# A 16-bit permutation turned by DMA transposes instead of TensorE, in a graph kernel whose engines run pair by pair

## The reference

```python
mask = (adj > 0.0).astype(x.dtype)
W1a, W1b = (W1[:F], W1[F:])
xj_proj = x @ W1a
diff = x[:, :, None, :] - x[:, None, :, :]
h = jax.nn.relu(xj_proj[:, :, None, :] + diff @ W1b + b1)
hm = jnp.einsum('bjkh,bjk->bjh', h, mask)
deg = jnp.sum(mask, axis=-1)
return hm @ W2 + deg[..., None] * b2
...
x = _layernorm(x + _L0_gnn_ref(x, adj, ...), axis=-1)
```

## Time and profile before

| | us |
|---|---|
| median of three runs | 252.81 |
| the profiled execution | 252.74 |
| its span, first to last instruction | 250.9 |
| PE busy | 235.9 (94%) |
| DVE busy | 226.6 (90%) |
| ACT busy | 209.8 (84%) |
| POOL busy | 121.4 (48%) |
| DMA, mean of 16 engines | 21.7% of the span |

### The profile page before, as it was taken

The page is one execution under the profiler, slowest core; times in us unless marked ns, Lnnn a source line. Parts: engine busy times, 40 slices in busy tenths (PEclk is TensorE's granted clock), DMA queues, the critical chain, the costliest instruction groups (busy, mean ns, idle before and its releaser), DMA issues. The chain is left out here.

```text
span 250.9 us, 9244 instructions
## 1 busy us (share of the span) xinstructions
PE 235.9 (94%) x2810; PEld 188.7 (75%) x2813; DVE 226.6 (90%) x778; ACT 209.8 (84%) x572; POOL 121.4 (48%) x288
## 2 busy tenths in 40 slices
PE   7947989999999999999999999999999999998992
PEld 2524758888787878787888878887878888886761
DVE  4757699999999999999999999999999999997763
ACT  2384888989998989899899999898999989987631
POOL 1124444363645637463736364563736483576225
PEclk9985899999999999999999999999999999999998
DMA  6983003221212213131313021221310110000002
GB/s 201 357 325 106 3 4 123 70 84 30 70 54 78 73 55 96 44 107 42 106 39 107 14 74 59 64 82 47 105 44 25 43 46 0 25 24 1 3 8 63
DMA packets 10550, 18.20 MB, mean 73 GB/s; under 512 B 1296, under 2 KB 7696, under 8 KB 10512
## 3 DMA queue, kind: packets, MB, share of 16 engines
q1 hardware_dynamic: 10512, 17.73, 21.7%
HBM read 15.63 MB, written 2.10 MB: 71 GB/s over the span
## 5 line engine op out<-in xcount | busy, mean ns | idle before, releaser
L1327 PE MATMUL ring<-hot,vh 128*128 128x128 bf16 (+9 forms) x768 | 117.4, 255 | 1.3 <-ACT ring L914 1.0
L1327 PE MATMUL ring<-hot,vl 128*128 128x128 bf16 (+9 forms) x768 | 116.3, 251 | 0.0
L1796 DVE SCALAR_TENSOR_TENSOR sums<-ring,sums 128x256 f32<-128x256 f32 (+10 forms) x240 | 97.8, 428 | 4.3 <-PE ring L1327 1.9
L1327 PEld LDWEIGHTS ring<-hot,vh 128*128 128x128 f16 (+1 forms) x768 | 62.0, 104 | 23.6 <-issue 16.8
L1327 PEld LDWEIGHTS ring<-hot,vl 128*128 128x128 f16 (+1 forms) x768 | 61.9, 103 | 2.4
L661 POOL TENSOR_TENSOR vl<-vf,vh 128x384 f16<-128x384 f32 x32 | 29.7, 929 | 63.2 <-ACT vf L870 59.4
L903 ACT COPY ring<-u_sb 128x192 f32<-128x192 f32 (+8 forms) x160 | 49.3, 359 | 7.4 <-DVE sums L1796 7.4
L900 ACT COPY ring<-u_sb 128x512 f32<-128x512 f32 (+1 forms) x80 | 43.3, 559 | 0.4 <-issue 0.2
L715 POOL TENSOR_TENSOR sums<-taken,sums 128x512 f32<-128x512 f32 x16 | 20.7, 1292 | 27.1 <-ACT taken L932 27.1
L821 ACT CAST maskT<-bx 128x512 bf16<-128x512 f32 x32 | 18.5, 586 | 14.3 <-PE bx L1171 13.8
L1771 DVE TENSOR_SCALAR hot<-slotT 128x944 bf16<-128x944 f16 (+6 forms) x112 | 28.6, 280 | 0.0
(11 more groups left out here) (119 smaller groups left out, 463.7 us busy)
## 6 DMA issues: line engine op xcount, KB each, us to landing
adj_sb<-adj SPq DMA_DIRECT2D x16, 512.0 KB, 3.7
x_sb<-x_pairs SPq DMA_DIRECT2D x16, 128.0 KB, 2.3
xT_sb<-xT SPq DMA_DIRECT2D x16, 128.0 KB, 2.1
x_all<-x SPq DMA_DIRECT2D x4, 512.0 KB, 7.9
out<-o_sb SPq DMA_DIRECT2D x16, 128.0 KB, 1.7
wts<-weights SPq DMA_DIRECT2D x1, 417.0 KB, 4.8
cst_general<-general SPq DMA_DIRECT2D x1, 256.0 KB, 3.2
cst_half<-half SPq DMA_DIRECT2D x1, 137.0 KB, 3.1
```

The costliest lines, as they stand in the source:

```text
L1327: return eng.matmul(to if part == "main" else to[g * HT:g * HT + HT], values, selection, start=False, stop=final, skip_group_check=True)
L1796: eng.scalar_tensor_tensor(out=to, in0=view(pair, part, unit, piece), scalar=0.0, in1=to, op0=ALU.max, op1=ALU.add).then_inc(added[part], 1)
```

## The change

DVE writes the permutation as bf16 (`perm16`), and `rank` is f16. ACT widens `perm16` to the f32 `perm` that `sort_x` needs (`widen_perm`, new). The four tiles of `perm16` are transposed by four DMAs, SBUF to SBUF, that SP issues with `transpose=True` into `permT16` (`turn_perm`, now on SP); ACT widens it to `permT` as before, now from SBUF. PE's `turn_perm`, the bf16 identity go. The PSUM bank `bx3` loses one user, so `project` and `excess_main` wait for `sums_started` where they waited for `permT_copied`. The orders of the tasks are changed on all five queues. The core of the diff:

```diff
-        rank = sb("rank", [P, TILES])
-        perm = both("perm", [P, TILES, P])
-        permT = both("permT", [P, TILES, P])
+        rank = sb("rank", [P, TILES], F16)
+        perm16, perm = both("perm16", [P, TILES, P], BF16), both("perm", [P, TILES, P])
+        permT16, permT = both("permT16", [P, TILES, P], BF16), both("permT", [P, TILES, P])
```

On SP:

```diff
+            def perm_to_turn(pair):
+                eng.wait_ge(perm_ready, pair.n + 1)
+
+            def turn_perm(pair):
+                for c in range(TILES):
+                    eng.dma_start(permT16[pair.side][:, c, :], perm16[pair.side][:, c, :],
+                                  transpose=True).then_inc(permT_landed[pair.side], 16)
...
             def body(pair, has=always):
+                if has(1):
+                    perm_to_turn(new)
+                if has(3):
+                    load_x(third)
+                if has(1):
+                    turn_perm(new)
                 if has(5):
                     load_adj(fifth)
                 if has(4):
                     load_xT(fourth)
-                if has(3):
-                    load_x(third)
                 if has(-1):
                     store(old)
```

On ACT:

```diff
+            def widen_perm(pair):
+                eng.wait_ge(perm_ready, pair.n + 1)
+                if pair.follows(2):
+                    eng.wait_ge(xs_ready, pair.n - 1)
+                eng.copy(perm[pair.side][:, :, :].rearrange("p c r -> p (c r)"),
+                         perm16[pair.side][:, :, :].rearrange("p c r -> p (c r)")).then_inc(perm_widened, 1)
...
             def copy_permT(pair):
-                eng.wait_ge(permT_ready, pair.n + 1)
+                eng.wait_ge(permT_landed[pair.side], 16 * TILES * (pair.half + 1))
...
                     full_v(pair, 0)
                 if has(-1):
+                    copy_permT(old)
                     seed(old, "main", 4)
...
                 if has(1):
+                    widen_perm(new)
                     copy_maskT(new, 0)
                     copy_maskT(new, 1)
                 if has(-1):
                     seed_joint(old)
-                if has(0):
-                    copy_permT(pair)
```

On PE:

```diff
             def sort_x(pair):
...
-                eng.wait_ge(perm_ready, pair.n + 1)
+                eng.wait_ge(perm_widened, pair.n + 1)
...
-            def turn_perm(pair):
...
-                eng.wait_ge(sums_started, pair.n + 1)
...
-                to = bx3.bitcast(BF16)
-                for c in range(TILES):
-                    last = eng.transpose(to[:, c * P:c * P + P], perm16(pair.side, c), ident[:, :])
-                last.then_inc(permT_ready, 1)
...
             def body(pair, has=always):
-                    gather(pair, "main", 6, 3, 4)
                     gather(pair, "tail", 3)
...
-                if has(2):
-                    turn_perm(second)
...
-                    gather(new, "main", 6, 0, 3)
+                    gather(new, "main", 6)
```

In the start-up of PE:

```diff
             hidden_u_main(Pair(0, 0))
             hidden_u_tail(Pair(0, 0))
+            excess_main(Pair(0, 0))
             spread_x()
+            set_banks(0)
             hidden_v(Pair(0, 0))
+            keys(Pair(0, 1))
             set_banks(1)
```

In the end of PE:

```diff
             gather(Pair(0, 15), "tail", 0)
+            gather(Pair(0, 15), "main", 0)
+            gather(Pair(0, 15), "main", 1)
             gather(Pair(0, 15), "tail", 1)
-            gather(Pair(0, 15), "main", 0)
-            keep_busy_last(7)
-            gather(Pair(0, 15), "main", 1)
...
+            project(Pair(0, 15))
+            unsort_y(Pair(0, 15))
             add_over()
-            project(Pair(0, 15))
+            keep_busy_last(7)
             keep_busy_last(2)
-            unsort_y(Pair(0, 15))
```

On DVE:

```diff
             def permutation(pair):
-                eng.tensor_tensor(perm[pair.side][:, :, :], places.unsqueeze(1).broadcast_to([P, TILES, P]),
+                eng.tensor_tensor(perm16[pair.side][:, :, :], places.unsqueeze(1).broadcast_to([P, TILES, P]),
                                   rank[:, :].unsqueeze(2).broadcast_to([P, TILES, P]), ALU.is_equal).then_inc(perm_ready, 1)
```

More of the change, by code:

```diff
@@ L433, in build @@
         general_step = sem("general_step")
-        def perm16(side, c):
-            return perm[side][:, c, :].bitcast(BF16).rearrange("p (r two) -> p r two", two=2)[:, :, 1]
         def bank(pair, part, unit):
@@ L558, in _ @@
             load_adj(Pair(0, 3))
+            perm_to_turn(Pair(0, 0))
             load_x(Pair(0, 2))
+            turn_perm(Pair(0, 0))
             load_xT(Pair(0, 2))
             load_adj(Pair(0, 4))
+            perm_to_turn(Pair(0, 1))
             load_x(Pair(0, 3))
+            turn_perm(Pair(0, 1))
             load_adj(Pair(0, 5))
@@ L572, in general @@
                 load_xT(pair)
+                perm_to_turn(pair)
                 load_x(pair)
+                turn_perm(pair)
                 store(pair)
@@ L740, in body @@
                     low_v(new, 0)
-                    low_v(new, 1)
                 if has(-2):
                     scale(older)
+                if has(1):
+                    low_v(new, 1)
                 if has(2):
@@ L877, in copy_permT @@
                 eng.copy(permT[pair.side][:, :, :].rearrange("p c n -> p (c n)"),
-                         bx3.bitcast(BF16)[:, 0:TILES * P]).then_inc(permT_copied, 1)
+                         permT16[pair.side][:, :, :].rearrange("p c n -> p (c n)")).then_inc(permT_copied, 1)
             def copy_y(pair):
@@ L1097, in general @@
             def general(pair):
+                widen_perm(pair)
                 for g in range(2):
@@ L1171, in turn_masks @@
                         last = eng.matmul((bx1, bx2)[g][:, at:at + P], mask[pair.side][:, g * NT + t, k * P:k * P + P],
-                                          perm16(pair.side, g * NT + t), start=True, stop=True)
+                                          perm16[pair.side][:, g * NT + t, :], start=True, stop=True)
                 last.then_inc(maskT_ready, 1)
@@ L1191, in number_slots @@
                             last = eng.matmul(b[:, at:at + P], least[pair.side][:, g, t * (NT + 1):t * (NT + 1) + 1].to_broadcast([P, P]),
-                                              perm16(pair.side, c), start=False, stop=True)
+                                              perm16[pair.side][:, c, :], start=False, stop=True)
                 last.then_inc(slots_ready, 1)
@@ L1282, in project @@
                         eng.wait_ge(z_added, PAIRS - 1)
-                    eng.wait_ge(permT_copied, pair.n + (1 if pair.last() else 2))
+                    eng.wait_ge(sums_started, pair.n + (1 if pair.last() else 2))
                 for step in range(first, end):
@@ L1484, in _ @@
             gather(Pair(0, 0), "main", 5)
-            turn_perm(Pair(0, 1))
             number_slots(Pair(0, 2), 0)
@@ L1566, in general @@
                 eng.wait_ge(general_step, (pair.data + 1) * (N * GENERAL_STEPS))
-                turn_perm(pair)
                 project(pair)
@@ L1642, in ranks @@
                         eng.wait_ge(above_ready, pair.n)
-                eng.tensor_reduce(rank[:, :], steps_ahead[:, :, :], AX.X, ALU.add).then_inc(ranks_ready, 1)
+                with nc.allow_low_precision(reason="whole numbers of at most 128"):
+                    eng.tensor_reduce(rank[:, :], steps_ahead[:, :, :], AX.X, ALU.add).then_inc(ranks_ready, 1)
             def permutation(pair):
@@ L1899, in body @@
                     select(old, 9)
+                if has(-2):
+                    add(older, "tail", 7)
                 if has(0):
@@ L1946, in body @@
                     masks(second)
+            first_max()
             masks(Pair(0, 0))
```

236 lines of the change are left out of this document (112 added, 124 removed).

## The result

The changed kernel takes 257.29 us (median of four runs, 257.15 to 257.61) against 253.03 for the kernel before in the same comparison: 1.0164 times as long, with a 95% interval of 1.0132 to 1.0196. That is 4.3 us slower. The forecast was 250.6 with a range of 248.6 to 254.8, and faster was the likeliest sign. The prediction was wrong, in sign too.

The account below looks back on a forecast made before the run. It took PE as going at its own pace, 13.60 us busy of 13.6 per pair, with DVE less than 1% behind. Terms -2.3 + 0 + 0.3 + 0 + 0.5 - 0.7 = -2.2 us gave 250.6, range 248.6 to 254.8.

Parts of the forecast that it names:

- Part 1: PE in the steady stretch: losing `turn_perm` frees 0.22 us a pair, 0.18 taken, -2.3 us (1.4 to 2.9 gained).
- Part 2: DVE's `permutation` writing 16 bits: no change from 686 ns, term 0, bound 0.27 us a pair.
- Part 3: ACT's `widen_perm` and moved `copy_permT`: +0.56 us work a pair, mostly hidden; +0.3 us, between 0 and 3.3.
- Part 4: DMA transposes on SP's queue: 0.5 us each plus 2.3 landing, 4.3 us within a 7.5 us window; cost 0.
- Part 5: Start-up and end: reordered start +0.5 us (-0.4 to +1.1); end without seven matmuls of ones -0.7 (0 to -1.3).
- Rival 1: DVE is the bound and PE's gain is not let through: only 1.4 us gained, 251.7 us; chance 0.24.
- Rival 2: Transposes land late, ACT waits at `copy_permT`; decides from 1.4 us each, 256.7 us at 1.5 each; chance 0.10.
- rival 3: ACT's places cost more than PE's time: 0.25 us delay a pair reaches `turn_masks`, 254.6 us; chance 0.13.

Follow-up runs that it names:

- e3: Kernel before without PE's four transposes per pair, ACT's copy waiting for `start_sums` instead: 0.9991 of the kernel before, median 253.09 us.
- e5: Kernel before with the new permutation mechanism alone, old orders, DMA transposes issued early, ahead of two other loads: 1.0015 of the kernel before, 253.31 us.
- e16: As e5, with pair 2 turned behind the load of x of pair 3 in the start-up: 0.9991 of the kernel before, 252.71 us.
- e1: Changed kernel with `first_max` put back behind `count_masks` in DVE's start-up: 1.0084 of the kernel before, median 255.36 us.
- e12: Changed kernel with the DMA transposes issued one body earlier on SP: 1.0098 of the kernel before, median 255.83 us.
- e14: Changed kernel with `first_max` back, PE's old end order and transposes one body earlier: 1.0063 of the kernel before, median 254.09 us.
- e15: Changed kernel with transposes one body earlier and `copy_permT` back behind `seed_joint`: 1.0581 of the kernel before, 266.91 us, period 13.64.
- e7: Kernel before without PE's four transposes and with half of one DVE add left out per pair: 0.9981 of the kernel before, 251.97 us.
- e10: Kernel before without four matmuls of main gather unit 1 and half of one DVE add per pair: 0.9898 of the kernel before, 251.04 us.
- e4: Kernel before with the new mechanism alone, old orders, DMA transposes issued behind the load of xT: 1.0473 of the kernel before, 264.80 us.
- e2: Changed kernel with the last part of PE's list as before, seven matmuls of ones included: 1.0108 of the kernel before, median 255.66 us.
- e8: Changed kernel with `first_max` back in its place and PE's last part as before: 1.0095 of the kernel before, median 254.93 us.

## Why the prediction was wrong

| term | forecast | measured |
|---|---|---|
| Part 1, PE loses `turn_perm` | -2.3 | 0: `e3` -0.2 of a total that tells 0.6, period +0.02 |
| Part 2, 16-bit `permutation` | 0 | 0: 689 ns, was 686 |
| Part 3, ACT | +0.3 | 0: `e5`, `e16` level with `e3` (13.60 and 13.62) |
| Part 4, transposes on SP | 0 | +0.8 in the ten periods of this execution, 0 to 1.5 in others: lateness |
| Part 5, start-up | +0.5 | +1.2 up to pair 3, a point that scatters by as much; `first_max` by the totals 2.0 (`e1`) |
| Part 5, end | -0.7 | +1.6, and +0.4 in the two periods ahead of it |
| new orders of the bodies otherwise | no term | +0.3 to +0.5 in ten periods (`e12`, `e14`, `e15` against `e16`) |

**The step that failed first is Part 1.** It said that time taken from PE alone is worth what DVE's slack lets through, at least the 0.11 us of DVE's empty time. PE had 13.60 us busy in a period of 13.6, so I took every microsecond on its list to be on the path. (The waits that I read as PE's, "issue", stand on a row of its weight load; PE itself had none. And the 0.39 us of rows 4 is four records together, one is 0.22; the 0.22 us of the list for all four stand.) A full engine is not a path, though: in the part of the list between `turn_masks` and gather 6, PE was busy with work that filled a wait it would have had anyway. That wait was invisible before for just that reason. `e3` showed it by taking the work out: 0.9991 of the time before (0.9967 to 1.0015), a gather that waits 0.20 us for `seed_joint`, and a period of 13.62. Zero should have been the lower end of that term, and a rival of its own.

**Rival 1** (DVE lets nothing through) still let 1.4 us through, and its mechanism was half of it. Relieving DVE as well (`e7`) did not free PE's time. It took the relief at the right place too (`e10`). Rival 2's 256.7 lies nearest to the measured 257.3, but that is luck: lateness was 0.8 of the 4.4 us.

**Part 2** was right, and so was its reading of the rows.

**Part 3** was right within its uncertainty. ACT's two copies of 0.52 us, start to start, were absorbed; rival 3 (ACT's places) is refuted by `e15`'s period and by `e16`.

**Part 4** had the mechanism right and two sizes wrong. I took 0.5 us of the queue for each transpose; it was 1.23, and 2.4 to land. A landing counts from the start of its own issue, so four are there after 3 x 1.23 + 2.4 = 6.1 us, as `e4` shows (6.12), not 4.3. And the window was not 7.5 us: in the changed kernel it was 6.9 (97.25 to the copy at 104.15, which did not wait) and 6.75 (111.32 to 118.07, from where the copy waited 0.49). A group of four at 4.9 us of the queue fits into that, and the one of 6.05 does not. My point from which rival 2 decides, 1.4 us each, had both faults in it: it put the landing behind the end of the last issue, and took the window of before. So a part of rival 2 was real, 0 to 1.5 us. Its full price is what `e4` shows. The Trainium skill's figure for one DMA transpose, 1309 ns (VectorE: DVE Perf Modes, "The three transpose paths"), is near the 1233 ns for which the row has the queue held, and below the 2.4 us to landing; I worked out 5.2 us from it, an estimate that also lies below the 6.1 measured, and did not carry it into the sum.

**Part 5** missed both ends. In the start-up I priced the moves of `masks`, `set_banks` and `widen_perm`, but not `first_max`, whose move I had noted. Its data comes over a DMA issued behind four others, and everything DVE does in the start-up stands behind it. In the end I credited the removal of seven matmuls of ones with 0.7 us. It gained nothing: at a high clock the end took 24.39 and 24.30 us without them, 24.34 with them (`e2`) and 23.85 before. And without any of them ahead of the last `unsort_y`, that ran at the lower clock in this execution and took 0.83 more; that their absence is the cause isn't shown.

The forecast said what would show rival 1: empty time on DVE of zero at a period above 13.55. It was not so after (1.7 us from 64 to 200 us). It said for rival 2 that `permT` heads ACT's waits; it was in the list once. So the page after pointed at none of the rivals in the steady stretch; only kernels that took one thing away did.

## What to carry to other kernels

Work that is removed from a fully busy engine is worth what it is worth at its place. Before pricing it, ask what the next instruction on that engine that waits for another engine would do if it came earlier by that much: here the gather would have waited for `seed_joint`. A transpose by DMA is not free where its issue holds a queue: count the queue's time for each, add one landing from the start of the last issue, and issue it as early as its source allows; the old orders with early transposes are level with the kernel before, and the same mechanism a few microseconds later cost 11 us. In a reordered list look first at its very first entries and at what the last matmuls find in front of them.

## What the runs showed of the hardware

- A 128x128 bf16 transpose by DMA from SBUF to SBUF held SP's queue for 1.09 to 2.33 us, 1.23 in the median, and landed 2.2 to 4.3 us after its issue. Four in a row took 4.9 us of the queue in the later rounds of the hardware loop and 5.0 to 6.2 elsewhere in the changed kernel (6.4 once in `e8`); I have no cause for that. At 4.9 they were there 6.1 us after the first issue.
- The same eight f32 matmuls took 1.10 us at the full clock and 1.93 at the lower one (granted clock 0.54 around them).
- ACT copied 128x512 from bf16 in SBUF to f32 in SBUF in 631 ns, against 576 for the same copy out of a PSUM bank before.
- Removing 0.22 us of PE and 0.26 of DVE from every pair changed nothing that could be measured (0.9981, 0.9951 to 1.0011).
